# A graph layer's source one-hots on Trainium2: compared with a tensor in place of a scalar per partition

## The reference

```python
agg = jax.ops.segment_sum(x[src], dst, num_segments=n) * deg_inv
h = agg @ Wl.T + bl + x @ Wr.T
norm = jnp.maximum(jnp.linalg.norm(h, axis=-1, keepdims=True), EPS)
return jax.nn.relu(h / norm)
```

## Time and profile before

| what | value |
|---|---|
| median of 3 runs (lowest to highest) | 7910.08 us (7909.2 to 7927.37) |
| profiled execution: its own time, its span | 7941.06 us, 7939.0 us |
| busy over the span: PE, DVE, ACT, POOL | 84%, 53%, 27%, 76% |
| edge network and middle stage, up to the first layer | 0 to about 5430 us |
| edge loop of layer 0, first gather to last | 5455.4 to 6532.5 us |
| edge loop of layer 1, first gather to last | 6669.6 to 7754.4 us |

### The profile page before, as it was taken

One profiled execution on the slowest core, in us unless ns is written; L12 is line 12 of the kernel. 1 busy time (PEld: TensorE's weight loads), 2 busy tenths in 40 slices (PEclk: granted clock), 3 DMA queues, 4 the chain that ended last, 5 costly groups with the idle time before them and its releaser, 6 DMA issues. The chain is left out here.

```text
span 7939.0 us, 139237 instructions
## 1 busy us (share of the span) xinstructions
PE 6681.0 (84%) x39214; PEld 5228.7 (66%) x39430; DVE 4236.9 (53%) x16294; ACT 2139.5 (27%) x4708; POOL 6022.3 (76%) x4866
## 2 busy tenths in 40 slices
PE   5889988899988998989889888796888876888883
PEld 4778877778777777878777777664444444444442
DVE  5777777777777743333333333334555554555553
ACT  2222222222222222222222222243333324333333
POOL 5888888888888888888888888734777775777783
PEclk7777777776777766676676667667999996999995
DMA  4333333333333332222222222232222223222221
GB/s 129 34 34 34 34 35 34 34 34 34 34 34 34 34 29 27 27 28 27 27 27 27 27 27 27 28 93 71 66 64 66 65 55 78 65 64 65 65 62 51
DMA packets 710748, 363.73 MB, mean 46 GB/s; under 512 B 552256, under 2 KB 658148, under 8 KB 710194
## 3 DMA queue, kind: packets, MB, share of 16 engines
q0 software_dynamic: 325280, 163.91, 20.1%
q1 hardware_dynamic: 382948, 195.00, 10.1%
q10 hardware_dynamic: 2286, 1.95, 0.1%
HBM read 279.51 MB, written 80.96 MB: 45 GB/s over the span
## 5 line engine op out<-in xcount | busy, mean ns | idle before, releaser
L664 POOL DMA_INDIRECT future<-sbuf,sidx x1564 | 2489.2, 1592 | 484.3 <-issue 457.0
L650 POOL DMA_INDIRECT gbuf<-in_x_dram,gidx x1564 | 1592.2, 1018 | 481.5 <-issue 472.2
L1537 PE MATMUL bank<-at_dst,rows 128*128 128x512 bf16 x2744 | 1084.8, 395 | 15.0 <-issue 3.3
L1389 POOL DMA_INDIRECT gb<-x,nidx x728 | 855.3, 1175 | 283.3 <-issue 168.0
L1389 POOL DMA_INDIRECT gb<-h,nidx x728 | 862.4, 1185 | 262.1 <-issue 170.1
L1502 ACT CAST rows<-bank 128x384 bf16<-128x384 f32 x1372 | 657.2, 479 | 1497.7 <-PE bank L1521 1497.0
L1535 PE MATMUL bank<-at_dst,rows 128*128 128x512 bf16 x2528 | 1002.8, 397 | 0.0
L976 PEld LDWEIGHTS bank<-w1pe,featT 96*128 96x128 f32 x3128 | 723.3, 269 | 306.1 <-issue 305.6
L1427 DVE TENSOR_SCALAR at_dst<-iota,metaf 128x512 bf16<-128x512 f16 x2744 | 827.3, 352 | 7.3 <-PE bank L1537 5.3
L977 PE MATMUL bank<-w1px,srcT 65*128 65x128 f32 x3128 | 816.5, 354 | 0.0
L976 PE MATMUL bank<-w1pe,featT 96*128 96x128 f32 x3128 | 816.4, 354 | 0.0
(11 more groups left out here) (260 smaller groups left out, 11464.5 us busy)
## 6 DMA issues: line engine op xcount, KB each, us to landing
laneb<-lanes SPq DMA_DIRECT2D x392, 224.0 KB
gbuf<-in_x_dram,gidx POOLq DMA_INDIRECT x1564
comb<-in_edge_attr_dram SPq DMA_DIRECT2D x391, 64.0 KB
future<-sbuf,sidx POOLq DMA_INDIRECT x1564, 3.2
blkb<-blkrow SPq DMA_DIRECT2D x210, 98.0 KB
future<-zero POOLq DMA_DIRECT2D x16, 800.0 KB, 17.8
fut<-future SPq DMA_DIRECT2D x100, 125.0 KB
gb<-x,nidx POOLq DMA_INDIRECT x732, 2.6
```

The costliest lines, as they stand in the source:

```text
L650: pool.indirect_dma_start(out=gbuf[:, b, q, :], out_offset=None, in_=x[:, :], in_offset=bass.IndirectOffsetOnAxis(ap=gidx[:, b, q:q + 1], ...
L664: pool.indirect_dma_start(out=future[q][:, :], out_offset=bass.IndirectOffsetOnAxis(ap=sidx[:, b, q:q + 1], axis=0), in_=sbuf[:, b, q, :], ...
L1389: pool.indirect_dma_start(out=gb1[:, m, q, :], out_offset=None, in_=frm[:, :], in_offset=bass.IndirectOffsetOnAxis(ap=nidx[:, i % 2, m, q: ...
L1537: pe.matmul(psL[i % 2][:, :], rows16[:, j % AR, t % 2, 2 * D:4 * D], at_dst[:, t % DR, :], start=(b == 0), stop=(b == BLOCKS - 1)).then_in ...
```

## The change

The comparison with `lane1` as a scalar per partition becomes a comparison of two tensors, in which `lane1` is read along the row with a step of zero; source and destination are named as flat rows of 896. Waits, semaphores, buffers, the order on DVE and the values made are as before.

```diff
-                        dve.tensor_scalar(at_src[:, k % 2, :, :], laneb[:, k % 3, :, :], lane1[:, 0:1], None,
-                                          ALU.is_equal).then_inc(t_src, 1)
+                        dve.tensor_tensor(at_src[:, k % 2, :, :].rearrange("p r n -> p (r n)"),
+                                          laneb[:, k % 3, :, :].rearrange("p r n -> p (r n)"),
+                                          lane1[:, 0:1].to_broadcast([P, RING * P]), ALU.is_equal).then_inc(t_src, 1)
```

## The result

The change made the kernel slower: 8078.86 us median of four runs (8073.15 to 8091.41) against 7909.64 (7908.77 to 7927.37), a ratio of 1.0211 with a 95% interval of 1.0192 to 1.0230. That is 169 us; the forecast was 31, and the range ended at 8000.

A forecast was written before the change was run, and what follows sets the result against it. The prediction took POOL's back-to-back gathers to bound the edge loops. It summed -60 (gain), +90 (loss) and +1.2 (loop starts) to +31 us on the 7910 median: 7941 us, range 7850 to 8000.

The forecast's parts named there:

- The instruction: at_src comparison on DVE: 1.08 us in place of 0.468, 239 us more DVE work, costed at nothing in the loop.
- Its cover: DVE's 908.8 us of waiting for PE's sums, 2.7 us at a time, was to absorb 0.66 us more a group.
- What is queued behind it: at_dst comparisons, next oneh and adds on DVE, and lane loads on SP's queue: later, but costing nothing.
- The start's 1.2 us: Start of each of two loops, where PE waits for the first at_src: 0.61 us later each, +1.2 us.
- The gain: POOL's gathers near their end, no longer held by at_src in two-tensor form: -60 us.
- what POOL loses: POOL's gathers near their start, held by the two-tensor at_src until it ends: +90 us, 125 the upper end.
- a discount of 28%: Cut on the 125 us of held starts, as some gathers would be held anyway: 331.6 us beside 1175.3 of DVE.
- A: Gathers starting within at_src: the two-tensor form holds none, only the gain is left, 7851 us; chance 0.25.
- B: Held starts get through when at_src ends, despite queued at_dst; gain and loss cancel, 7910 us; chance 0.27.
- C: Freed gathers run into the next hold, so no gain: 8001 us, or 8036 undiscounted; chance 0.07 beyond the forecast's neighbourhood.
- D: Two-tensor at_src takes no more than 0.61 us, so held starts cost 15 us: 7865 us; chance 0.03.

The follow-up runs named there:

- the run with the memset and the form with the sum: Kernel before with at_src as a scalar comparison that also writes its row sum, and a 128x896 memset ahead of it: 7834.4 us, ratio 0.9920.
- the two-byte run: The change's two-tensor comparison, with the lane numbers as a dense f16 row of 896, against the kernel before: 7991.1 us, ratio 1.0114.
- the change with breaks: The change plus a memset of two columns ahead of every at_dst, against the kernel before: 7768.7 us, ratio 0.9813.
- the first profile: Profile of the unchanged kernel before that the prediction used: execution 7941.06 us, span 7939.0 us, gathers 1717.7 us.
- the one with the sum: Kernel before with at_src as a scalar comparison that also writes its row sum, which nothing reads: 7858.3 us, ratio 0.9934.
- the second's: Second profile, from running the unchanged kernel before again: 7874.6 us, span 7872.7 us, gathers 1647.9 us.
- the run with the extra memset: Kernel before with a 128x896 memset into an unread tile ahead of the plain scalar at_src: 7988.4 us, ratio 1.0094.
- the two kernels with breaks: A two-column memset ahead of every at_dst, on the kernel before (7670.5 us, ratio 0.9676) and on the change (7768.7 us, ratio 0.9813).

## Why the prediction was wrong

The bound was read right: POOL goes from gather to gather with 0.30 us between, and the loops grew by 139.2 us where the gathers grew by 140.1.

The instruction was priced right: 1.086 us for 1.08. Its cover held: DVE still waits 787.3 us for PE's sums, and 0.7 us more a chunk cost nothing in the run with the memset and the form with the sum. What is queued behind it cost nothing that the trace shows. The start's 1.2 us is too small to be seen.

The gain had the right sign, but its size is not settled: 60 us were forecast, and the excess of the others fell by 83 or by 13 us, by which profile of before is taken. Leaving at_src out gave 100, with the 27 of the gathers begun under it and with a break at every chunk. In the two-byte run the gain did not come at all.

The step that failed is what POOL loses: +90 us forecast, 250 - 27 = 223 by the gathers begun under at_src. Its mechanism up to at_src's end was right: 0.73 starts a comparison make 286, 279 were counted, and the hold until at_src's end grew by 131 - 7 = 124 us where 125 was written. That so close a match came out is luck: 154 was written for the 131 and 29 for the 7, and the two errors cancel. Then the 125 were cut to 90 by a discount of 28%, for gathers that would be held anyway; the 124 that were measured leave no room for it. And the step let every gather go when the comparison ends. It had no term for a train that takes the hold over: 119 - 20 = 99 us more, of which the change with breaks has next to nothing. Against the first profile the terms add up, 124 + 99 - 83 = 140 us, the growth of the gathers. The range missed for the missing term, since its upper end was the discounted loss with no gain; even 125 with no gain, 8036, would have been too low. So the mean gather, 1.276 us, lies beyond every case that was listed (1.14 to 1.24).

Of the rivals, A fell: a two-tensor form does hold gathers. B's mechanism was there for 137 gathers, which got away at at_src's end, but 84 others were held on, and no saving shows. C, "the loss alone", came nearest, for another reason than it gave: by the first profile the gain was there, and the loss over twice the size. D fell with the length, 1.086 us; and the two-byte form, which has D's 0.61 us, took 7991 us where D's sum gave 7865.

The Trainium skill, page "SBUF — State Buffer", section "Who interferes with whom", bears on it from both sides. Its rule that an instruction with two SBUF inputs contends with what GpSimd reads, that one with a single input outside the two-port modes does not, and that the scalar form which writes its accumulator stays out of those modes agrees with the runs: 250 us of excess under the two-tensor form, 37 under the one with the sum, 11 of them until its end, and none under the memset with that form behind it. Its inference that a tensor_tensor leaves descriptor generation alone does not carry over to a whole gather here: 233 of the 279 begun under one were held at their start, and they go on beside it when they got in before it, as that of 5475.73. What the gather does in its held part, no run here shows.

## What to carry to other kernels

Where POOL's indirect DMAs set the pace, choose the form of a DVE instruction by what it does to them and not by its own length: of forms of at_src of 1.1 us, one made the kernel 0.7% faster and another 2.1% slower. Look in the timeline for gathers that take two or three times their median, and at what DVE does until 0.1 or 0.8 us before they end. A run of scalar comparisons on DVE that stands back to back can be broken by a two-column memset: 165 us more on DVE took 280 us off the gathers of the first profile (210 off the second's) and 3.2% off the kernel.

## What the runs showed that was not expected

A break of 0.060 us between two scalar comparisons lets a waiting gather through; most of the holds of this kernel, 280 of 332 us, are gone with it, and the prediction had taken the comparisons' length for the cause, sharing the excess out by time. A gather that begins while a harmless instruction runs can still be held, by the plain scalar comparison queued behind it: 147 of 167 in the run with the extra memset. And the kernel before is itself unsteady by this: its two profiles differ by 70 us in gather time with nothing changed, and its runs of one set spread over up to 53 us, while the runs of each of the two kernels with breaks lie within 12 us of each other.
